# Neighbourhood attention with the scores of two heads issued together, one 512-column filler a unit, and a shorter choice chain

## The chip, the core and the metric

The kernel runs on one core of one Trainium2 chip. The metric is the device time of one execution in microseconds, from three runs of the kernel before. One more execution was recorded by the hardware profiler; the rows further down are from it. Engines are PE (TensorE), DVE (VectorE), ACT (ScalarE), POOL (GpSimd) and SP (which issues most DMAs). Each works through its own queue in order and waits on semaphores.

## The reference

The input is 2 images of 32 x 32 positions with 64 channels. Three layers follow each other:

```python
# 1: neighbourhood attention, 4 heads of 16 channels, a window of 7 x 7 keys, then an MLP
x = x + proj(softmax(q @ k_window + bias) @ v_window)
x = x + gelu(layernorm(x) @ fc1 + b1) @ fc2 + b2
# 2: global attention over 1024 tokens, 8 heads of 64
t = t + softmax(q @ k.T) @ v @ Wu + bu
# 3: 33 steps; op is the largest of the first 19 entries of token 0 of image 0
for step in range(33):
    op = argmax(h[0, 0, :19])
    h = where(attn_mask[step, op], attention(h; wq, wk, wv, wo of (step, op)), h)
    h = where(ffn_mask[step, op], relu(h @ w1 + b1) @ w2 + b2, h)
```

## The kernel before

**The neighbourhood loop.** A unit is one tile of 128 queries and one head: 2 images x 8 tiles x 4 heads = 64 units. The keys of a tile are up to 10 rows of 32 positions (320 columns; 224 for the first and last tile of an image). Each engine runs its own loop over steps i, software-pipelined by hand:

- PE, step i: `nat_score(i + 2)` (L663): wait until DVE has biased unit i (so one of the two score banks, PSUM 0 and 1, is free), one filler matmul of 256 columns (`keep_busy`, L658, L661), then two score matmuls in a 32-row group of the array (high and low part of the queries, L675). Then `nat_turn(i - 1)` (L680): wait for the exponentials, one filler, two or three 128x128 transposes of the probabilities (L688) into bank 4 for even and bank 5 for odd units. In steps 2 modulo 4 come the value sums of a tile (`nat_values`, L691, L702), in steps 0 modulo 4 the projection (`nat_project`, L707, L711), because `LAG_SUM, LAG_DRAIN, LAG_PROJ, LAG_WEIGH = 6, 7, 8, 9`.
- DVE, step i: bias and minimum of unit i in one instruction (L1520), for odd i then the copy of the transposes of unit i - 2 (L318), in steps 1 modulo 4 then the weighing of a tile's heads (L1452, L1456), and then its share of the side work.
- ACT, step i: the exponential of unit i (L1097), for even i the copy of the transposes of unit i - 2, and in steps 3 modulo 4 the copy of the value sums (L1106).

Side work stands in the same steps by a table `at_step`: on PE `x` 9, `q` 12, `k` 15, `v` 19, `wT` 24, `wk` 27, `mix` 30, `wu` 33, `y` 47, `h` 49, `H` 51, `mlp` 53 to 56, `a` 65, each drained by ACT or DVE a step or so later (10, 13, 16, 20, 25, 28, 31, 34, 48, 50, 52, 57, 66). The mean and variance of a layer norm take DVE six small instructions, one a step: steps 1 to 6, 40 to 45, and 58 to 63; POOL then raises to the power -1/2 (L1287) and DVE divides at steps 8, 46 and 64.

**The filler.** It multiplies the identity matrix, read as 16-bit numbers, by itself into a bank that is overwritten next. Its result is used by nobody.

**The global stage.** Four pairs of heads with 32 steps each (`glob_pair`); PE runs scores (L807), transposes (L820) and value sums (L834). In the first pair some work of the stage before is done beside (`rest_of_stage1`).

**The choice.** For each update of the third layer PE puts token 0 in a row of PSUM (`show_row`, L881) and `choose` (L1663) on DVE finds the operation and the next step at which a mask is set for it: twelve chained instructions, each waiting for the one before, among them two over all 33 x 19 = 627 codes (L1679, L1682), and then two that write the control words. All engines wait for these in `scan` (L370). The table of codes is made by four chained instructions (L1658 to L1661) after the last global pair, before the moments of the next layer norm. With this input there are two updates (the first an FFN alone, the second an attention and an FFN), and `choose` runs three times.

Of the kernel before, what the change touches and what calls it, by code (L numbers as in the profile page):

```python
# [67 lines left out]
NCTL = 12  # L68
# [38 lines left out]
def build(nc, a, out):  # L107
    ctx = ExitStack()
    with ctx:
# [82 lines left out]
        code = sb("code", [1, NSTEP])  # L192
        key = sb("key", [1, NSTEP])
        dead = sb("dead", [1, NSTEP])
        row = sb("row", [1, C])
# [174 lines left out]
        def scan(e, attend, feed, after):  # L370
# [13 lines left out]
            def update():  # L384
# [3 lines left out]
                slot = e.snap(nu, min_val=0, max_val=NSTEP - 1)  # L388
                if attend:
                    with e.If(flags >= 2):  # L390
                        attend(e.snap(na, min_val=0, max_val=NSTEP - 1), step, slot)
                        e.reg_add(na, na, 1)
# [63 lines left out]
        MLP_STEPS, ADD_STEP, DIVIDE_STEP, INPUT_STEP = 4, 3, 6, 7  # L456
# [78 lines left out]
        def _(pe):  # L535
# [831 lines left out]
        def _(dve):  # L1367
# [219 lines left out]
            def rest_of_stage1(i):  # L1587
# [55 lines left out]

            glob_pair(0, prev=False, beside=rest_of_stage1)
# [5 lines left out]
            cn = [0]  # L1650

            def link(ins):
                cn[0] += 1
                ins.then_inc(codes_made, 1)
                dve.wait_ge(codes_made, cn[0])
            dve.wait_ge(late_loaded, 32)
            dve.wait_ge(consts_made, 4)
            link(dve.tensor_copy(codes[:, :, :], mask8[:, 0, :, :]))  # L1658
            link(dve.tensor_copy(codew[:, :, :], mask8[:, 1, :, :]))
# [199 lines left out]
```

## Time and profile before

| | us |
|---|---|
| median of 3 runs | 726.95 |
| lowest, highest | 723.34, 731.72 |
| profiled execution | 727.6 |
| its span, first to last instruction | 725.7 |
| PE busy | 636.4 (88% of the span) |
| DVE busy | 465.6 (64%) |
| ACT busy | 386.7 (53%) |
| mean granted TensorE clock, share of 2.4 GHz | 0.939 |

Busy time counts an engine's instructions, not its waits. Matmuls are pipelined, so a PE record is longer than the time to the next record; where it matters, the distance from start to start is the one to take. A wait is put down to the instruction that came last before it ended.

### The profile page before, as it was taken

Reading aid. Unit: us, or ns where it says so; the run is one execution under the profiler, and the core shown is the slowest. Engines: PE = TensorE matmul, PEld = TensorE weight load, DVE = VectorE, ACT = ScalarE, POOL = GpSimd, SP = SyncE. Lnnn points to the kernel's source line nnn. Section 1 sums busy time; section 2 is a strip of 40 time slices with the busy share of each in tenths; the row PEclk is TensorE's granted clock in tenths of the full one; section 3 lists DMA queues with packets and bytes.
Section 4 is the critical chain, followed back from the end, with each engine's and each line's share of the span. In section 5 each row is a group of like instructions: output and inputs, shape, how many; then the busy total and the mean of one; then the engine's idle time right before and its main releaser. Section 6 shows DMA issues by size and latency. Waiting matters only on the chain.

```text
span 725.7 us, 11085 instructions
## 1 busy us (share of the span) xinstructions
PE 636.4 (88%) x3951; PEld 348.2 (48%) x3952; DVE 465.6 (64%) x799; ACT 386.7 (53%) x683; POOL 50.3 (7%) x100
## 2 busy tenths in 40 slices
PE   7999999959789999999999999999999656279961
PEld 5555655525445555555555555555555321147621
DVE  5655464553966676767677666766676454599743
ACT  3534557335666666666666666666565204355430
POOL 5021323130000000000000000000000000000000
PEclk9999999876999999999999999999999886699986
DMA  4000000000000000000000000000000000000001
GB/s 96 1 1 1 2 1 1 1 0 1 1 0 1 1 1 1 1 1 1 0 1 0 0 0 0 0 1 1 0 1 1 0 8 3 12 1 2 1 0 30
DMA packets 9509, 3.24 MB, mean 4 GB/s; under 512 B 8820, under 2 KB 9079, under 8 KB 9463
## 3 DMA queue, kind: packets, MB, share of 16 engines
q1 hardware_dynamic: 8182, 2.61, 1.6%
q8 instruction: 30, 0.49, 0.3%
q10 hardware_dynamic: 1281, 0.01, 0.1%
q14 instruction: 16, 0.13, 0.1%
HBM read 2.09 MB, written 0.52 MB: 4 GB/s over the span
## 4 chain that ended last, share of the span: by engine, by line
PE 74%; DVE 12%; issue 9%; ACT 2%; POOL 2%; DMA 1%; SPq 0%; DVEq 0%; POOLq 0%; ACTq 0%
PE PS L834 16%; PE PS L807 15%; PE PS L820 13%; PE PS L661 3%; PE PS L675 3%; PE PS L688 2%; PE PS L860 2%; PE PS L515 2%; PE PS L767 2%; PE PS L702 2%; PE PS L487 2%; PE PS L959 2%; PE PS L499 2%; DVE negm L1608 2%; PE PS L561 1%
## 5 line engine op out<-in xcount | busy, mean ns | idle before, releaser
L1608 DVE TENSOR_REDUCE negm<-PS 128x1 f32<-128x1024 f32 x128 | 156.6, 1223 | 120.2 <-PE PS L807 120.2
L1168 ACT ACTIVATE prob<-PS,negm 128x1024 f32<-128x1024 f32 x128 | 143.0, 1117 | 43.9 <-DVE negm L1608 43.9
L820 PE MATMUL PS<-ident,prob 128*128 128x128 f32 x1024 | 135.9, 274 | 10.5 <-DVE PT L1620 10.3
L820 PEld LDWEIGHTS PS<-ident,prob 128*128 128x128 f32 x1024 | 119.9, 141 | 39.0 <-DVE PT L1620 13.2
L834 PE MATMUL PS<-PT,V 128*64 128x512 f32 x512 | 134.3, 617 | 0.0
L807 PE MATMUL PS<-aS,qS 128*128 128x512 f16 x512 | 133.9, 384 | 0.0
L1180 ACT ACTIVATE PT<-PS 128x512 f32<-128x512 f32 x128 | 76.6, 598 | 106.8 <-PE PS L820 106.2
L807 PEld LDWEIGHTS PS<-aS,qS 128*128 128x128 f16 x512 | 44.7, 99 | 95.7 <-issue 52.1
L1620 DVE COPY PT<-PS 128x512 f32<-128x512 f32 x128 | 87.2, 681 | 5.2 <-PE PS L820 5.2
L1097 ACT ACTIVATE prob<-sbias,negm 128x320 f32<-128x320 f32 (+1 forms) x64 | 34.3, 537 | 38.0 <-DVE negm L1520 37.4
L1287 POOL TENSOR_TENSOR rstd<-var,minus_half 128x8 f32<-128x8 f32 x8 | 13.2, 1646 | 468.0 <-DVE var L1391 468.0
L661 PE MATMUL PS<-ident 128*128 128x256 f16 x128 | 39.3, 307 | 5.4 <-DVE negm L1520 4.1
L834 PEld LDWEIGHTS PS<-PT,V 128*64 128x64 f32 x512 | 27.3, 135 | 30.0 <-issue 29.8
L318 DVE COPY PT<-PS 128x384 f32<-128x384 f32 (+1 forms) x32 | 16.7, 523 | 33.6 <-PE PS L688 33.6
L1520 DVE CUSTOM_DVE_ANT_0 sbias<-PS,PT 128x320 f32<-128x320 f32 (+1 forms) x64 | 28.8, 459 | 7.7 <-PE PS L675 7.6
L688 PE MATMUL PS<-ident,prob 128*128 128x128 f32 x176 | 33.5, 299 | 0.0
L675 PE MATMUL PS<-k0S,q0S 32*128 32x320 f16 (+1 forms) x128 | 30.4, 322 | 0.0
L661 PEld LDWEIGHTS PS<-ident 128*128 128x128 f16 x128 | 13.1, 103 | 33.5 <-issue 16.6
L1000 ACT ACTIVATE prob<-PS,negm 128x1024 f32<-128x1024 f32 x16 | 17.8, 1115 | 20.5 <-DVE negm L1345 20.5
L1142 ACT ACTIVATE qS<-PS 128x512 f16<-128x512 f32 x36 | 21.2, 599 | 8.4 <-PE PS L767 7.9
L1168 ACT ACTIVATION_READ_ACCUMULATOR prob<-PS,negm 128x1 f32 x128 | 25.3, 198 | 0.0
L767 PE MATMUL PS<-aS,wqk 128*128 128x512 f16 x64 | 20.4, 414 | 5.0 <-DVE qS L1576 3.6
(175 smaller groups left out, 688.9 us busy)
## 6 DMA issues: line engine op xcount, KB each, us to landing
xall<-in_x_dram SPq DMA_DIRECT2D x2, 256.0 KB, 4.4
out_dram<-x SPq DMA_DIRECT2D x4, 128.0 KB, 2.1
w<-in_L_attn_Wq_dram SPq DMA_DIRECT2D x2, 128.0 KB, 2.5
w<-in_L_attn_Wk_dram SPq DMA_DIRECT2D x2, 128.0 KB, 2.6
w<-in_L_attn_Wv_dram SPq DMA_DIRECT2D x2, 128.0 KB, 2.7
fc<-in_L_conv_fc_w_dram SPq DMA_DIRECT2D x2, 64.0 KB, 2.5
wu<-in_L_attn_Wu_dram SPq DMA_DIRECT2D x2, 64.0 KB, 2.4
w1s<-in_L_ffn_ffn_w_dram SPq DMA_DIRECT2D x2, 64.0 KB, 2.1
```

The lines of the kernel that those rows point to most:

```text
L661: pe.matmul(bank[:, 0:FILL], filler[:, 0:P], filler[:, 0:FILL], start=True, stop=True)
L675: mm = pe.matmul(PS[:, u % 2, 0:rows * WW], q0S[hr, img, part, t * P:(t + 1) * P], k0S[hr, img, first * WW:(first + rows) * WW], start=(pa ...
L688: tr = pe.transpose(bank[:, n * P:(n + 1) * P], prob[:, u % 3, n * P:(n + 1) * P], ident[:, :])
L767: m = pe.matmul(bank, w.rearrange("p h a c -> p (h a c)"), aS[:, blk * BLK:(blk + 1) * BLK], start=(part == 0), stop=(part == 1))
L807: mm = pe.matmul(scores2[i % 2][:, j * BLK:(j + 1) * BLK], qS[:, part, lane, q0:q0 + P], aS[:, k0 + j * BLK:k0 + (j + 1) * BLK], start=(pa ...
L820: tr = pe.transpose(bank[:, k * P:(k + 1) * P], prob[:, u % 4, kt * P:(kt + 1) * P], ident[:, :])
L834: mm = pe.matmul(OB[cols, :], V[:, g % GP // 2 * NT + kt, cols], PT[:, g % 2, lane, kt, :], start=(kt == 0), stop=(kt == NT - 1))
L1097: act.activation(prob[:, i % 3, 0:w], sbias[:, i % 3, 0:w], ACT.Exp, bias=negm[:, i % 4:i % 4 + 1], scale=-1.0).then_inc(c0["exped"], 1)
L1168: act.activation(prob[:, i % 4, :], scores2[i % 2], ACT.Exp, bias=negm[:, i % 4:i % 4 + 1], scale=1.0, accum_out=sums[:, i // GRP, (i % GR ...
L1180: act.activation(PT[:, g % 2, lane, 0:4, qt * P:(qt + 1) * P], LO.rearrange("p (k q) -> p k q", k=4), ACT.Copy).then_inc(c1["lo_drained"], 1)
L1608: dve.tensor_reduce(negm[:, i % 4:i % 4 + 1], scores2[i % 2], AX.X, ALU.max, negate=True)\
L1620: dve.tensor_copy(PT[:, g % 2, lane, 4:8, qt * P:(qt + 1) * P], HI.rearrange("p (k q) -> p k q", k=4)).then_inc(c1["hi_drained"], 1)
```

## The change

- In the neighbourhood loop PE issues the scores of units u and u + 1 together, in steps with even i: high part of both heads, then low part of both. The heads lie in different 32-row groups and write different banks. Before them PE waits until DVE has biased both units before (`biased` >= u instead of u - 1). The filler ahead of the scores is gone.
- The filler ahead of each unit's transposes has 512 columns instead of 256.
- `choose` reads the row where it lies in PSUM, and has five chained instructions instead of twelve. It picks from a row of 19 prepared next keys (`nextkey`) instead of from all 627 codes.
- That row is made for the first choice by `key_table`, seven instructions in steps 17 to 23 of the first global pair on DVE, which also take the place of the four that made the codes after the last pair. For each later choice it is made by `keys_left`, three chained instructions on DVE (19x33 elements twice) that `scan` places at the start of every update, before its attention and FFN.

```diff
-NCTL = 12
+NCTL, NAHEAD = 5, 3
...
                 slot = e.snap(nu, min_val=0, max_val=NSTEP - 1)
+                if ahead:
+                    ahead(slot)
...
-        MLP_STEPS, ADD_STEP, DIVIDE_STEP, INPUT_STEP = 4, 3, 6, 7
+        MLP_STEPS, ADD_STEP, DIVIDE_STEP, INPUT_STEP, KEY_STEP = 4, 3, 6, 7, 17
...
-                pe.matmul(bank[:, 0:FILL], filler[:, 0:P], filler[:, 0:FILL], start=True, stop=True)
-
-            def nat_score(u):
-                T, h = u // NH0, u % NH0
+                pe.matmul(bank[:, 0:2 * FILL], filler[:, 0:P],
+                          filler.rearrange("p (o n) -> p o n", o=1).to_broadcast([P, 2, FILL]), start=True, stop=True)
+
+            def nat_scores(u):
+
+                T = u // NH0
...
                 if u >= 2:
-                    pe.wait_ge(c0["biased"], u - 1)
+                    pe.wait_ge(c0["biased"], u)
...
-                keep_busy(PS[:, u % 2, :])
-                hr = slice(32 * h, 32 * h + 32)
                 for part in range(2):
-                    mm = pe.matmul(PS[:, u % 2, 0:rows * WW], q0S[hr, img, part, t * P:(t + 1) * P],
-                                   k0S[hr, img, first * WW:(first + rows) * WW],
-                                   start=(part == 0), stop=(part == 1))
-                mm.then_inc(c0["scored"], 1)
+                    for n in range(2):
+                        hr = slice(32 * ((u + n) % NH0), 32 * ((u + n) % NH0) + 32)
+                        mm = pe.matmul(PS[:, n, 0:rows * WW], q0S[hr, img, part, t * P:(t + 1) * P],
+                                       k0S[hr, img, first * WW:(first + rows) * WW],
+                                       start=(part == 0), stop=(part == 1))
+                        if part == 1:
+                            mm.then_inc(c0["scored"], 1)
...
-            nat_score(0)
-            nat_score(1)
+            nat_scores(0)
             for i in range(UN0 + LAG_PROJ - NH0 + 1):
-                if i + 2 < UN0:
-                    nat_score(i + 2)
+                if i % 2 == 0 and i + 2 < UN0:
+                    nat_scores(i + 2)
...
+                if 0 <= i - KEY_STEP < 7:
+                    key_table(i - KEY_STEP)
...
+            def key_table(n):
...
+                if n == 0:
+                    ins = dve.tensor_copy(codes[:, :, :], mask8[:, 0, :, :])
+                elif n == 1:
+                    ins = dve.tensor_copy(codew[:, :, :], mask8[:, 1, :, :])
+                elif n == 2:
+                    ins = dve.scalar_tensor_tensor(codes[:, :, :], codes[:, :, :], 2.0, codew[:, :, :],
+                                                   ALU.mult, ALU.add)
+                elif n == 3:
+                    ins = dve.tensor_scalar(codew[:, :, :], codes[:, :, :], 0.0, float(NONE), ALU.is_equal, ALU.mult)
+                elif n == 4:
+                    ins = dve.tensor_tensor(codes[:, :, :], codes[:, :, :], steps, ALU.add)
+                elif n == 5:
+                    ins = dve.tensor_tensor(codes[:, :, :], codes[:, :, :], codew[:, :, :], ALU.max)
+                else:
+                    ins = dve.tensor_reduce(nextkey[:, :], by_op(codes), AX.X, ALU.min)
...
+            def keys_left(slot):
+
+                base = slot * (NCTL + NAHEAD) + NCTL
+                dve.tensor_scalar(dead[:, :], steps4[:, :], nextf[:, 0:1], float(NONE), ALU.is_le, ALU.mult)\
+                   .then_inc(ctl_chain, 1)
+                dve.wait_ge(ctl_chain, base + 1)
+                dve.tensor_tensor(codew[:, :, :], codes[:, :, :],
+                                  dead[:, :].rearrange("p (s o) -> p s o", o=1).to_broadcast([1, NSTEP, NOPS]),
+                                  ALU.max).then_inc(ctl_chain, 1)
+                dve.wait_ge(ctl_chain, base + 2)
+                dve.tensor_reduce(nextkey[:, :], by_op(codew), AX.X, ALU.min).then_inc(ctl_chain, 1)
+                dve.wait_ge(ctl_chain, base + NAHEAD)
...
-            link(dve.tensor_copy(codes[:, :, :], mask8[:, 0, :, :]))
-            link(dve.tensor_copy(codew[:, :, :], mask8[:, 1, :, :]))
-            link(dve.scalar_tensor_tensor(codes[:, :, :], codes[:, :, :], 2.0, codew[:, :, :], ALU.mult, ALU.add))
-            link(dve.memset(nextf[:, :], -4.0))
...
-                link(dve.tensor_copy(row[:, :], bank[0:1, 0:C]))
-                link(dve.tensor_reduce(top[:, :], row[:, 0:NOPS], AX.X, ALU.max))
+                row = bank[0:1, 0:NOPS]
+                link(dve.tensor_reduce(top[:, :], row, AX.X, ALU.max))
+
+                link(dve.scalar_tensor_tensor(cand[:, :], row, top[:, 0:1], opfrac[:, :], ALU.is_lt, ALU.add))
                 link(dve.tensor_reduce(opf[:, :], cand[:, :], AX.X, ALU.min))
-                link(dve.scalar_tensor_tensor(
-                    codew[:, :, :], opfrac[:, :].rearrange("p (o n) -> p o n", o=1).to_broadcast([1, NSTEP, NOPS]),
-                    opf[:, 0:1], codes[:, :, :], ALU.is_equal, ALU.mult))
-                link(dve.tensor_reduce(code[:, :], codew[:, :, :], AX.X, ALU.add))
...
-                link(dve.tensor_reduce(nextf[:, :], key[:, :], AX.X, ALU.min))
+                link(dve.scalar_tensor_tensor(cand[:, :], opfrac[:, :], opf[:, 0:1], nextkey[:, :],
+                                              ALU.is_equal, ALU.mult))
+                link(dve.tensor_reduce(nextf[:, :], cand[:, :], AX.X, ALU.add))
...
-            scan(dve, attend, feed, choose)
+            scan(dve, attend, feed, choose, keys_left)
```

## Rows read from the trace of the kernel before

**Rows 1.** Stretch, us: busy PE, PEld, DVE, ACT, POOL (x instructions), PEclk, DMA share, GB/s

```profile
24.00:152.00 128.00, 120.23 (x951) 67.59 (x952) 70.30 (x229) 64.08 (x136) 32.34 (x71) 0.96 0.01 1
```

**Rows 2.** Waits, 24 to 152: total us, times, longest us

```profile
DVE PT L318 <- PE PS L688: 33.6, 26, 3.1
...
PE PS L661 <- DVE negm L1520: 4.1, 9, 1.0
```

**Rows 3.** Timeline of PE, 69 to 75: start us, us, engine, line, operation

```profile
69.04 0.60 PE L711 MATMUL PS<-pw,OT 128*128 128x260 f32 x2
...
69.69 0.44 PE L675 MATMUL PS<-k0S,q0S 32*128 32x320 f16 x2
...
70.06 0.28 PE L661 MATMUL PS<-ident 128*128 128x256 f16 x1
...
70.81 0.28 PE L661 MATMUL PS<-ident 128*128 128x256 f16 x1
...
71.94 1.00 PE L702 MATMUL PS<-PT 128*32 128x128 f32 x24
...
74.49 0.28 PE L661 MATMUL PS<-ident 128*128 128x256 f16 x1
...
74.61 0.49 PE L688 MATMUL PS<-ident,prob 128*128 128x128 f32 x3
...
74.93 0.60 PE L711 MATMUL PS<-pw,OT 128*128 128x260 f32 x2
```

**Rows 4.** Timeline of DVE in the same stretch

```profile
69.25 0.56 DVE L318 COPY PT<-PS 128x384 f32<-128x384 f32 x1
...
69.72 0.17 DVE L1452 RECIPROCAL rinv<-PS 128x4 f32<-128x4 f32 x1
...
70.27 0.48 DVE L1520 CUSTOM_DVE_ANT_0 sbias<-PS,PT 128x320 f32<-128x320 f32 x1
...
70.67 0.48 DVE L1520 CUSTOM_DVE_ANT_0 sbias<-PS,PT 128x320 f32<-128x320 f32 x1
```

**Rows 5.** Timeline of PE, 33 to 43: the same score records, four units apart

```profile
33.35 0.71 PE L675 MATMUL PS<-k0S,q0S 32*128 32x320 f16 x2
...
42.62 0.71 PE L675 MATMUL PS<-k0S,q0S 32*128 32x320 f16 x2
```

**Rows 6.** A fall of the clock: timeline of PE at 135, and the stretch behind it

```profile
135.19 0.28 PE L661 MATMUL PS<-ident 128*128 128x256 f16 x1 [0.96 <-DVE negm L1520]
...
135.00:143.00 8.00, 7.81 (x51) 4.14 (x51) 3.91 (x15) 3.01 (x7) 0.30 (x1) 0.57 0.01 2
```

**Rows 7.** Timeline of PE: side matmuls on fixed rows, and on alternating halves

```profile
86.32 1.10 PE L615 MATMUL PS<-PT 64*128 64x64 f32 x8
...
90.41 0.68 PE L628 MATMUL PS<-wu,PT 64*64 64x64 f32 x16
```

**Rows 8.** Timeline of DVE: two side instructions between biases

```profile
101.82 0.69 DVE L1385 TENSOR_TENSOR xn<-xall,mean 128x512 f32<-128x512 f32 x1
...
109.31 0.95 DVE L1407 TENSOR_TENSOR xn<-xn,rstd 128x512 f32<-128x512 f32 x1 [1.37 <-POOL rstd L1287]
```

**Rows 9.** Timeline of DVE: the second choice

```profile
617.55 0.21 DVE L1673 COPY row<-PS 1x64 f32<-1x64 f32 x1 [0.63 <-PE PS L881]
...
619.34 0.80 DVE L1682 TENSOR_REDUCE code<-codew 1x33 f32<-1x627 f32 x1
...
621.63 0.14 DVE L1691 TENSOR_SCALAR control<-opf 1x1 f32 x1 [0.16 <-DVE nextf L1689]
```

**Rows 10.** Timeline, 563 to 603: the table of codes, and the first update's split

```profile
563.00 0.46 DVE L1658 CAST codes<-mask 1x627 f32<-1x627 uint8 x1
...
564.95 0.69 DVE L1381 TENSOR_REDUCE mean<-x 128x8 f32<-128x512 f32 x1
...
571.32 0.47 PE L820 MATMUL PS<-ident,prob 128*128 128x128 f32 x1 [5.93 <-DVE PT L1620]
...
602.68 0.87 DVE L1748 TENSOR_TENSOR w1S<-w1s,w1S 64x256 f16<-64x256 f32 x2 [1.94 <-ACT w1S L1227]
```

More of the change, by code:

```diff
@@ L191, in build @@
         codew = sb("codew", [1, NSTEP, NOPS])
-        code = sb("code", [1, NSTEP])
-        key = sb("key", [1, NSTEP])
         dead = sb("dead", [1, NSTEP])
-        row = sb("row", [1, C])
+        nextkey = sb("nextkey", [1, NOPS])
         top = sb("top", [1, 1])
@@ L364, in build, with scan @@
         LN2_STEP, LN3_STEP = SUM_STEP + LN + 1, at_step["mlp", 0][1] + LN + 1
-        def scan(e, attend, feed, after):
+        def scan(e, attend, feed, after, ahead=None):
             word = e.alloc_register("word")
@@ L1642, in glob_pair @@
                         beside(i)
+            by_op = lambda t: t[:, :, :].rearrange("p s n -> p n s")
+            def key_table(n):
+                if n == 0:
+                    dve.wait_ge(late_loaded, 32)
+                    dve.wait_ge(consts_made, 4)
+                else:
+                    dve.wait_ge(codes_made, n)
+                steps = steps4[:, :].rearrange("p (s o) -> p s o", o=1).to_broadcast([1, NSTEP, NOPS])
+                if n == 0:
+                    ins = dve.tensor_copy(codes[:, :, :], mask8[:, 0, :, :])
[10 more added lines that the diff above has]
+                    ins = dve.tensor_tensor(codes[:, :, :], codes[:, :, :], codew[:, :, :], ALU.max)
+                else:
+                    ins = dve.tensor_reduce(nextkey[:, :], by_op(codes), AX.X, ALU.min)
+                ins.then_inc(codes_made, 1)
+            def keys_left(slot):
[9 more added lines that the diff above has]
+                dve.wait_ge(ctl_chain, base + NAHEAD)
             glob_pair(0, prev=False, beside=rest_of_stage1)
@@ L1647, in _ @@
             glob_pair(NPAIR - 1, last=True)
[L1650 to L1657, printed above, removed]
-            link(dve.tensor_copy(codes[:, :, :], mask8[:, 0, :, :]))
-            link(dve.tensor_copy(codew[:, :, :], mask8[:, 1, :, :]))
-            link(dve.scalar_tensor_tensor(codes[:, :, :], codes[:, :, :], 2.0, codew[:, :, :], ALU.mult, ALU.add))
-            link(dve.memset(nextf[:, :], -4.0))
             def choose(now, bank=YB):
-                base = now * NCTL
+                base = now * (NCTL + NAHEAD)
                 n = [0]
@@ L1672, in choose @@
                 dve.wait_ge(row_turned, now + 1)
-                link(dve.tensor_copy(row[:, :], bank[0:1, 0:C]))
-                link(dve.tensor_reduce(top[:, :], row[:, 0:NOPS], AX.X, ALU.max))
-                link(dve.scalar_tensor_tensor(cand[:, :], row[:, 0:NOPS], top[:, 0:1], opfrac[:, :],
-                                              ALU.is_lt, ALU.add))
+                row = bank[0:1, 0:NOPS]
+                link(dve.tensor_reduce(top[:, :], row, AX.X, ALU.max))
+                link(dve.scalar_tensor_tensor(cand[:, :], row, top[:, 0:1], opfrac[:, :], ALU.is_lt, ALU.add))
                 link(dve.tensor_reduce(opf[:, :], cand[:, :], AX.X, ALU.min))
-                link(dve.scalar_tensor_tensor(
-                    codew[:, :, :], opfrac[:, :].rearrange("p (o n) -> p o n", o=1).to_broadcast([1, NSTEP, NOPS]),
-                    opf[:, 0:1], codes[:, :, :], ALU.is_equal, ALU.mult))
-                link(dve.tensor_reduce(code[:, :], codew[:, :, :], AX.X, ALU.add))
-                link(dve.tensor_scalar(dead[:, :], steps4[:, :], nextf[:, 0:1], float(NONE), ALU.is_le, ALU.mult))
-                link(dve.tensor_scalar(key[:, :], code[:, :], 0.0, float(NONE), ALU.is_equal, ALU.mult))
-                link(dve.tensor_tensor(key[:, :], key[:, :], dead[:, :], ALU.max))
-                link(dve.tensor_tensor(code[:, :], code[:, :], steps4[:, :], ALU.add))
-                link(dve.tensor_tensor(key[:, :], key[:, :], code[:, :], ALU.max))
-                link(dve.tensor_reduce(nextf[:, :], key[:, :], AX.X, ALU.min))
+                link(dve.scalar_tensor_tensor(cand[:, :], opfrac[:, :], opf[:, 0:1], nextkey[:, :],
+                                              ALU.is_equal, ALU.mult))
+                link(dve.tensor_reduce(nextf[:, :], cand[:, :], AX.X, ALU.add))
                 assert n[0] == NCTL
@@ L1709, in _ @@
                 if i == STATE_STEPS[1]:
+                    dve.wait_ge(codes_made, 7)
                     choose(0, PS[:, 2, :])
```

## The prediction

> **What bounds the kernel now.** I read the busy times by stage first. In the neighbourhood stage, 24 to 152 us, PE is busy 120.2 of 128 us and DVE 70.3 [rows 1]; the global stage is PE work too, and the change leaves its PE program alone. So the first question is whether PE waits in the neighbourhood stage, and for whom. The waits say: hardly; before its fillers it stood 4.1 us in all for the bias (DVE), while DVE stood 33.6 us in 26 waits for the transposes before its copies [rows 2]. PE is the bound there, with DVE close behind.
>
> The timeline of PE and of DVE over four units (one key tile: one projection, one value sum) shows how close [rows 3, 4]. From projection to projection 5.89 us pass. A filler with its transposes holds PE 0.44 (74.49 to 74.93); a score pair takes 0.37 until the next filler starts (69.69 to 70.06). On DVE, copy to next instruction is 0.47, the two head-weighing instructions take 0.55, and two biases follow each other at 0.40 and last 0.48.
>
> **The neighbourhood loop, part by part.** Before, a unit's PE work is filler, scores, filler, transposes. Now steps with i even issue the scores of two heads at once, and only turns carry a filler, twice as long. The number of filler columns stays. What changes is the wait: the pair may start only when DVE has biased both units before it, so the two banks are never one ahead of the other. I follow one block of four units (i = 0 to 3 modulo 4, from the moment the bias of unit i+1 is done); DVE's copy of an odd unit stands before the next bias in its queue, and the transposes it needs now stand behind the new scores in PE's.
>
> First leg, i = 0: release 0.06 (the first bias ends at 70.75, the filler that waits for it starts at 70.81), scores 0.42, transposes done after a longer filler 0.12 + 0.11 + 0.49 = 0.72, DVE copy 0.47 starting at 1.24. The projection starts on PE at 1.04 and is ready at 1.64, DVE weighs from 1.71 to 2.26, two biases (0.40 + 0.48 + a short read-out, 0.91) end at 3.17. Second leg, i = 2: 0.06 + 0.42 + 0.72 + 0.04 + copy 0.47 + biases 0.91 = 2.62; PE meanwhile does scores 0.48, turn 0.66, values about 0.95, turn 0.56 = 2.65. Together 5.8, against 5.9 before [rows 3, 4]. At the high clock I count the block of bare units as 0: PE's saving turns into a PE gap of about 1.0 us in the first leg, and DVE with its hand-over becomes the bound.
>
> At the low clock the same legs give 4.4 + 3.9 = 8.3 us (streaming counted twice: scores 0.64, turn 1.05, projection 0.86, values 1.0) where the block takes 9.27 (33.35 to 42.62; the score record is 0.71 there and 0.44 later [rows 3, 5]). Three such blocks: -3.0.
>
> Side work on PE that stands in steps 0 or 1 modulo 4 now falls into the 1.0 us gap: folded values (0.68), weight turning, one hidden block, two quarters of the MLP, each between that and the 1.10 of the mixing or longer [rows 7]; five at 0.85, as the gap allows: -4.2. The query projections are there too, but DVE waits for them at once: 0.
>
> Side work on DVE is the counterpart. Before, an instruction of moments, drains or divides between two biases hid under PE if it stood in step 2, 3 or 0; now each such instruction delays a pair. The moments are busy 0.69 each, of which the next instruction overlaps a little, the drains 0.8; I take 0.65 as the mean. I count sixteen large ones by the step tables (moments 3, 4, 42, 43, 44, 58, 60, 62; divides 8, 46; drains 10, 16 twice, 20 twice, 48): 16 x 0.65 = 10.4. The wait of 1.37 for POOL at step 46 now stands in the path too: 11.8 [rows 8]. Less 1.8 that PE already stood for them (4.1 of rows 2, less about 0.28 in eight blocks): +10.0.
>
> Loop: -3.0 - 4.2 + 10.0 = +2.8. Bounds: DVE's part fully hidden -7; fully added with no gain from gaps +12.
>
> Do the two heads really overlap? The trace has no two score records in different row groups. Nearest: the sixteen 64x64 matmuls that alternate between both halves of rows and columns take 0.68 in all, 0.04 each, where eight on fixed rows take 1.10, 0.14 each [rows 7]. So disjoint parts overlap; I take full overlap (0.42), and no overlap (0.42 + 0.27) as the other end, 0.27 = 2 x 320 columns at 2.4 GHz. The Trainium skill (TensorEngine Tiling (Array Packing), Key Properties) says that tiles in different rows can load weights and multiply in parallel and that changing the tiling mode drains the engine; with it the scores would be the 0.42 taken. The same page (PSUM Bottleneck) warns that tiling speeds up TensorE but not the PSUM evacuation, which may become the bound; that speaks against the change, and the legs above are how I read it here.
>
> **The choice chain.** Before, row copy to control word is 617.55 to 621.63 less 0.16, about 3.95 us. After: reduce 0.24 from PSUM, compare 0.27, reduce 0.19, a 19-wide select 0.26, reduce 0.19 = 1.15 [rows 9]. It runs three times; the first lies beside PE's last global value sums (0), the other two are alone on the path: 2 x 2.8 = -5.6. Reading the row in PSUM twice instead of once may cost 0.1 each; bound -5.0.
>
> What was left out of the chain comes back as three instructions at the start of each update, ahead of all DVE work: 0.27 + 0.83 + 0.83, plus waits and register work, 2.1 (the 627-element reduce is 0.80 [rows 9]; its new order of reading is unmeasured, between 0.80 and 1.6). In the first update DVE goes from its register work straight to the split of the FFN weights at 602.68, which PE waits for [rows 10]: +2.1. In the second update DVE stands for the loaded attention weights anyway: 0, at worst +2.1.
>
> The four instructions that made the code table stood at 563.00, before the moments at 564.95, and PE's next transposes at 571.32 waited 5.93 us for DVE behind them [rows 10]: -1.9. They move as seven instructions, about 4.7 us, to steps 17 to 23 of the first global pair, one a step of some 3 us in which PE is bound and DVE about two thirds busy: 0, at worst +1.5. Tail: -5.6 + 2.1 - 1.9 = -5.4.
>
> **Sum.** The profiled execution took 727.6 us (span 725.7), the median is 726.95, so the two can be read as one. 727.6 + 2.8 - 5.4 = 725.0.
>
> **Rivals.**
> - A, the clock falls in the gaps. PE now stands about 1.0 us in each block, more where DVE has side work in steps 1 and 2 (1.4 more at 57/58 and 61/62). Before, the granted clock fell to the 1.2 GHz level right after a stand of 0.96 us at 135.19, and averaged 0.57 over the next 8 us [rows 6]. A block costs 8.3 at the low level and 5.9 at the high: 2.4 more. If some 45 us are low, 45 / 8.3 x 2.4 = +13: 738. It decides (slower by 1%) from about 32 us of low clock. Against: fillers per turn are denser than before, and 47 to 135 us stayed high in spite of nine stands.
> - B, the row groups do not overlap: 32 pairs x 0.27 = +8.6: 733.6, slower but just within 1%.
> - C, the high clock comes early. Before, PE ran some 22 us at the low level though it never stood [rows 5]. The new PE stream is denser between its gaps. Three blocks at 5.9 rather than 8.3: -7, 718.
> - D, the side work on DVE hides after all (drains of other steps absorb it): 725 - 8 = 717.
> - E, the shortened choice isn't shorter on the path: the three returned instructions cost in both updates, with a slow reduce: +3: 728.
>
> **Chances.** Forecast with E 0.42 (720 to 732); A 0.20; B 0.13; C 0.15; D 0.10. The range leaves out the far ends of A and of C with D together: 714 to 742; the likeliest case by itself 720 to 732. A measurement of this kernel tells about 1% from no change, 719.7 to 734.2: faster 0.26 (C, D, a sliver), slower 0.27 (A, part of B), same 0.47.
>
> **What would show it.** In the neighbourhood stage: PE waits before the scores for the bias, about once a block, some 1 us and in all 15 to 30 us instead of 4.1; four score records followed by a filler within 0.45 (0.7 means B); DVE's waits for the transposes stay near 1 us. Score and filler records at the low level past 47 us mean A, at the high level before 40 mean C. The choice should take 1.2 us of DVE from first to last reduce; PE's stand at 571 should shrink to 4.0, the first FFN matmul should come 2.1 later against the state's turn. I am wrong above all if side work on DVE doesn't add, or if the clock goes another way.

## The result: 1.1% slower

| | before | after |
|---|---|---|
| median of 20 runs each, same chip, us | 723.51 | 732.33 |
| lowest, highest | 721.18, 731.75 | 727.91, 741.05 |
| ratio after / before | | 1.0111, 95% [1.0083, 1.0140] |
| profiled execution (its span) | 727.6 (725.7) | 730.34 (728.4) |
| PE busy | 636.4 | 619.6 |

Ratios here and below leave out the executions that lie over 1.5 per cent above the fastest of their kernel, the medians hold all, and so a ratio and the quotient of two medians differ by up to half a per cent.

I had forecast a gain of 2 us, to 725.0; measured is a loss of 8.8 between the medians. The time itself lies within 714 to 742, but the direction and the size do not match, and the loss is just beyond the 1% that I had called no change.

How the two profiled executions run apart, by the same places of the program (start, us; "behind" is after less before):

| place | before | after | behind |
|---|---|---|---|
| first matmul of the loop (a filler before, scores after) | 24.25 | 24.33 | +0.1 |
| first global projection piece (end of the neighbourhood stage) | 152.64 | 160.70 | +8.1 |
| moments after the global stage | 564.95 | 570.91 | +6.0 |
| first FFN matmul | 604.30 | 613.40 | +9.1 |
| second choice: first reduction | 617.79 | 626.26 | +8.5 |
| its control word | 621.63 | 627.50 | +5.9 |
| end of the span | 725.7 | 728.4 | +2.7 |

All that is lost is lost in the neighbourhood stage. Behind it the steps of the short choice come out as they were summed (below), but for 0.7 us between the moments and the first FFN matmul, where eight transposes took 1.81 us (581.92) for 1.10 before (575.98). One caution on this pair: the profiled execution of before is one of its longer ones, 4 us above its median, and that of after is 2 us below its own. So the stage's +8.1 understates the loss.

The neighbourhood stage of after, the view of [rows 1], with the stage's whole length (24 to 160.7) as a second row:

```profile
24.00:152.00 128.00, 100.76 (x827) 61.04 (x827) 63.39 (x213) 60.05 (x128) 26.92 (x62) 0.92 0.00 1
24.00:160.70 136.70, 106.19 (x889) 64.33 (x889) 69.50 (x229) 63.12 (x136) 31.79 (x71) 0.93 0.01 1
```

PE was busy 120.23 of 128 us; now it is 100.76, and over the whole, longer stage 106.19. It has some 14 us less to do and needs 8 us more for it. The clock is 0.92 where it was 0.96. The waits of the stage (24 to 162 us), the view of [rows 2], say where the time stands:

```profile
DVE PT L316 <- PE PS L691: 52.3, 30, 6.5
...
PE PS L677 <- DVE negm L1522: 25.3, 20, 3.5
```

PE's wait for the bias went from 4.1 us to 25.3, and DVE's wait for the transposes from 33.6 to 52.3. Each engine waits more for the other: neither is the bound, the hand-over between them is.

The score pair, in the timeline of PE (answering [rows 3]):

```profile
73.77 0.49 PE L691 MATMUL PS<-ident,prob 128*128 128x128 f32 x3
74.19 0.44 PE L677 MATMUL PS<-k0S,q0S 32*128 32x320 f16 x4
74.56 0.39 PE L661 MATMUL PS<-ident 128*128 128x512 f16 x1
74.79 0.49 PE L691 MATMUL PS<-ident,prob 128*128 128x128 f32 x3
75.12 0.60 PE L714 MATMUL PS<-pw,OT 128*128 128x260 f32 x2
```

Four score matmuls, then the filler 0.37 later (74.19 to 74.56), the distance that two took before (69.69 to 70.06, [rows 3]). The two row groups overlap fully. Rival B is out by this row.

### The profile page after: what moved, and what is told of

Same layout as the page of the kernel before. It is cut to its first block, busy times and chain, and to the rows that moved or that the text cites. A ratio compares the mean times of both kernels' runs of the same rounds, so it can differ in the third digit from the quotient of the medians.

```text
span 728.4 us, 10937 instructions
## 1 busy us (share of the span) xinstructions
PE 619.6 (85%) x3887; PEld 344.9 (47%) x3888; DVE 464.2 (64%) x787; ACT 385.0 (53%) x683; POOL 49.7 (7%) x100
## 4 chain that ended last, share of the span: by engine, by line
PE 70%; DVE 14%; issue 9%; ACT 3%; POOL 2%; DMA 1%; DVEq 0%; SPq 0%; POOLq 0%; ACTq 0%
PE PS L836 15%; PE PS L809 15%; PE PS L822 13%; PE PS L691 2%; PE PS L661 2%; PE PS L862 2%; PE PS L515 2%; PE PS L769 2%; DVE sbias L1522 2%; DVE negm L1612 2%; PE PS L677 2%; PE PS L487 2%; PE PS L499 2%; PE PS L705 2%; PE PS L561 1%
## 5 line engine op out<-in xcount | busy, mean ns | idle before, releaser
L822 PEld LDWEIGHTS PS<-ident,prob 128*128 128x128 f32 x1024 | 120.5, 142 | 37.4 <-DVE PT L1624 11.6
L316 DVE COPY PT<-PS 128x384 f32<-128x384 f32 (+1 forms) x32 | 16.8, 524 | 52.3 <-PE PS L691 52.3
L677 PE MATMUL PS<-k0S,q0S 32*128 32x320 f16 (+1 forms) x128 | 15.4, 322 | 25.8 <-DVE negm L1522 25.3
L691 PEld LDWEIGHTS PS<-ident,prob 128*128 128x128 f32 x176 | 26.7, 159 | 8.7 <-issue 3.7
L661 PE MATMUL PS<-ident 128*128 128x512 f16 x64 | 28.3, 443 | 1.2 <-ACT PT L316 0.8
L1170 ACT ACTIVATION_READ_ACCUMULATOR prob<-PS,negm 128x1 f32 x128 | 25.3, 197 | 0.0
L1578 DVE SCALAR_TENSOR_TENSOR qS<-PS,qS 128x512 f16<-128x512 f32 x36 | 24.3, 682 | 0.4 <-ACT qS L1144 0.3
```

Of the source, the lines that this page charges most:

```text
L661: pe.matmul(bank[:, 0:2 * FILL], filler[:, 0:P], filler.rearrange("p (o n) -> p o n", o=1).to_broadcast([P, 2, FILL]), start=True, stop=True)
L677: mm = pe.matmul(PS[:, n, 0:rows * WW], q0S[hr, img, part, t * P:(t + 1) * P], k0S[hr, img, first * WW:(first + rows) * WW], start=(part = ...
L691: tr = pe.transpose(bank[:, n * P:(n + 1) * P], prob[:, u % 3, n * P:(n + 1) * P], ident[:, :])
L822: tr = pe.transpose(bank[:, k * P:(k + 1) * P], prob[:, u % 4, kt * P:(kt + 1) * P], ident[:, :])
L1170: act.activation(prob[:, i % 4, :], scores2[i % 2], ACT.Exp, bias=negm[:, i % 4:i % 4 + 1], scale=1.0, accum_out=sums[:, i // GRP, (i % GR ...
```

## Experiments

The kernels of one group ran on one chip together with before; each ratio is to the runs of before beside it.

### Which part loses: one part alone

`e1` is before with the new attention order and filler, and the old choice. `e2` is before with the new choice alone. `e4` is before with only the filler's part:

```diff
 def nat_score(u):
     ...
-    keep_busy(PS[:, u % 2, :])
     ...
 def keep_busy(bank):
-    pe.matmul(bank[:, 0:FILL], filler[:, 0:P], filler[:, 0:FILL], start=True, stop=True)
+    pe.matmul(bank[:, 0:2 * FILL], filler[:, 0:P], filler.rearrange("p (o n) -> p o n", o=1).to_broadcast([P, 2, FILL]), start=True, stop=True)
```

`e3` is the changed kernel with one swap, so that the older unit's turn doesn't queue behind the pair's wait:

```diff
-    if i % 2 == 0 and i + 2 < UN0:
-        nat_scores(i + 2)
     if 1 <= i <= UN0:
         nat_turn(i - 1)
+    if i % 2 == 0 and i + 2 < UN0:
+        nat_scores(i + 2)
```

> The kernel before with the new score and filler part only, the choice as before. If the loss is all in the neighbourhood loop, this is slower than the full change: the loop's +8.0 us of the profiled executions and nothing given back, ratio to before 1.011 to 1.018. If the parts only cost together (rival: the clock falls because both move work), it is near 1.00 to 1.005.

> The kernel before with the choice part only. From the profile after: -2.8 for each of two choices, -1.9 for the code table, +2.4 for the three instructions ahead of the first update: -5.1 us, ratio 0.993. If the seven instructions in the first global pair or the three in the second update cost something, it is 0.996 to 1.00.

> The kernel after, with PE issuing in each even step the transposes of unit i - 1 before the two score pairs instead of behind them; nothing else is moved. Hand-over theory (DVE's copy of the odd unit waits for transposes that stand behind scores that wait for DVE's bias): both legs lose about 1.2 us of waiting, PE's waits before the scores fall from 25 us to under 8, DVE's before its copies from 52 to under 15, and the loop gets 12 to 20 us shorter: ratio to before 0.975 to 0.99. Clock theory (the loss is only the stretches at the low clock): the order of the issues matters little, ratio 1.00 to 1.015.

> The kernel before with the filler part only: 512 columns ahead of each unit's transposes, none ahead of the scores; scores one head at a time as before. Filler theory (the fillers' new place costs the clock): low-clock stretches appear between 47 and 135 us and the time grows, ratio above 1.005. Hand-over theory: the filler's place is no cause; PE saves the switch of the array ahead of each score pair, about 0.1 us a unit in a loop that PE bounds, 0 to -7 us, ratio 0.99 to 1.00.

| kernel | median | ratio to before | 95% |
|---|---|---|---|
| e1, new attention alone | 738.49 | 1.0179 | 1.0125 to 1.0233 |
| e2, new choice alone | 718.69 | 0.9923 | 0.9888 to 0.9959 |
| e4, filler alone | 718.90 | 0.9927 | 0.9901 to 0.9952 |
| e3, changed kernel, turn first | 715.15 | 0.9860 | 0.9813 to 0.9908 |

The parts add up: 1.0179 x 0.9923 = 1.0101, against 1.0111 for both. The choice gives 5.6 us, as summed. The attention costs 12.9 us where I had +2.8. Inside it the filler gives 5.3, so pairing the scores with its wait costs 1.0179 / 0.9927 = 1.025, about 18 us. And it is the order of turn and wait that costs: with the turn ahead of the wait, e3 comes to 0.986, which is within its interval what filler and choice give by themselves (0.9927 x 0.9923 = 0.985).

The waits fell less than I had expected. PE's wait for the bias came down from 25.3 to 13.3 us (expected under 8), DVE's for the transposes from 52.3 to 24.5 (under 15):

```profile
DVE PT L316 <- PE PS L691: 24.5, 14, 6.3
...
PE PS L677 <- DVE negm L1522: 13.3, 17, 2.9
```

The clock isn't what helped e3: over its loop (24 to 147.45) the mean is 0.90, below the 0.93 of the changed kernel.

### Does DVE's side work stand in line now, and did it not before?

`e5` and `e6` add the same work to before and to after, in steps 2 modulo 4:

```diff
+    if i < UN0 and i % 4 == 2:
+        dve.memset(scratch[:, :], 0.0)
```

> The kernel before, with one more instruction of DVE in every fourth step of the attention loop: a memset of 128x512 into a tile that nobody reads, 16 in all, ahead of the step's side work. Its length is taken as about 0.6 us, so some 9 us of added DVE work. Theory 'hand-over' (DVE's side work costs time only where TensorE has nothing but DVE's next result to go on with): before, every unit's scores have their own step of lead, TensorE waited for the bias 9 times for 4.1 us, so most of the 9 us disappear: 0 to +3 us (ratio 1.000 to 1.004). Rival 'DVE in line everywhere': +9 us (1.012), here as in the changed kernel. Rival 'DVE's side work never adds': 0 in both.

> The changed kernel with the same 16 memsets. Hand-over: the pair's scores wait for DVE, with the older unit's turn queued behind them, so the 9 us stand in line: +6 to +9 us over the changed kernel, 1.019 to 1.023 of the kernel before if the changed one stands at 1.011. Rival 'DVE's side work never adds': 1.011, and the loss of the change is then of the clock or of the order alone.

Groups of instructions by line on DVE in e6, with busy us and mean ns: the added work.

```profile
L1528 DVE MEMSET scratch<- 128x512 f32 x16 | 7.8, 485 | 0.9
```

Before with it: 722.75, ratio 1.0004 [0.9975, 1.0032]. After with it: 737.87, ratio 1.0203 [1.0160, 1.0246]. So 7.8 us of DVE work at this place are free in before, to within 2 us, and in after they cost 0.9 per cent, 6.7 us, known to about 4. The waits of PE for the bias show the same, first e5, then e6:

```profile
PE PS L662 <- DVE negm L1521: 4.0, 9, 1.0
```

```profile
PE PS L678 <- DVE negm L1523: 28.9, 20, 3.5
```

Before's row hasn't moved with 7.8 us more to do (4.1 in [rows 2]); after's rose from 25.3 to 28.9. A part of the 6.7 may be the clock, since the profiled loop of e6 has 0.88 for 0.93. One stretch of the loop is free of that: from tile 7's projection to tile 10's, with three of the memsets in it, first e5, then e6:

```profile
93.14:112.32 19.18, 17.83 (x164) 9.99 (x163) 14.79 (x46) 9.89 (x22) 6.10 (x13) 1.00 0.00 1
```

```profile
104.88:131.68 26.80, 16.28 (x152) 9.68 (x151) 15.34 (x47) 10.52 (x22) 6.09 (x13) 0.94 0.00 1
```

The same stretch takes 19.18 without the memsets in before's order and 25.80 at 0.93 in after (both rows stand below). So the old order hides all three, and of the 1.31 us that DVE does more in the new one 1.00 shows.

`e10` and `e11` go the other way: in both kernels the two reductions and the square of each set of moments in the loop are cut to 64 of 512 columns.

```diff
+    m = 1 if k in (2, 3, 4) else NT
-    ins = dve.tensor_tensor(xsq[:, :, :], buf, buf, ALU.mult)
+    ins = dve.tensor_tensor(xsq[:, 0:m, :], buf[:, 0:m, :], buf[:, 0:m, :], ALU.mult)
```

> The kernel before, where nine of DVE's side instructions in the attention loop (the two reductions and the square of the three sets of moments) do only the first 64 of their 512 columns, 0.68 us each before, about 0.15 then: some 4.8 us of DVE work left out, and the output is not the reference's. Hand-over theory: 0 to -2 us (0.997 to 1.000), as this work lies beside TensorE's. Rival (DVE is in line before too): -4.8 us, 0.993.

> The changed kernel with the same nine instructions cut to 64 columns (the output is not the reference's). Hand-over theory: the pair's wait passes DVE's side work on, so -3.5 to -5 us against the changed kernel, 1.004 to 1.006 of the kernel before if the changed one stands at 1.011. If the work hides, 1.011. If its absence also keeps the clock up, more than -5 us, below 1.004.

As whole times these two can't be compared: the wrong means reach the choice, and other updates are done, so that they take 657.67 and 660.10 us. What can be read is a stretch of the loop. In the same stretch, tile 7's projection to tile 10's (steps 36 to 48), lie three of the shortened instructions. It took, in e2 (before's order) and in e10:

```profile
95.11:114.29 19.18, 17.83 (x164) 9.99 (x163) 13.54 (x43) 9.83 (x22) 6.10 (x13) 1.00 0.00 1
```

```profile
90.28:109.47 19.19, 17.84 (x165) 10.01 (x164) 12.34 (x43) 9.74 (x22) 6.11 (x13) 1.00 0.00 1
```

and in after and e11:

```profile
93.65:119.45 25.80, 16.23 (x152) 9.48 (x151) 14.03 (x44) 10.48 (x23) 6.09 (x13) 0.93 0.01 1
```

```profile
96.21:120.65 24.44, 16.28 (x153) 9.68 (x151) 12.61 (x44) 10.21 (x23) 6.10 (x13) 0.93 0.01 1
```

DVE's busy time falls by 1.20 in the old order and the stretch stays at 19.2; in the new one it falls by 1.42 and the stretch by 1.36. At equal clocks in each couple that is the same answer as e5 and e6: side work is hidden in the old order and stands in line, nearly whole, in the new one. Not everywhere, though: e10's first projection came at 39.81 instead of 41.41, so the early moments had cost before something too.

### How much of it is the clock?

After's stretch from tile 11's projection to tile 13's, and the same work in e11 and e2:

```profile
127.89:151.13 23.24, 19.18 (x135) 13.64 (x133) 9.14 (x29) 10.01 (x19) 2.82 (x8) 0.71 0.00 1
```

```profile
129.08:146.05 16.97, 12.98 (x135) 9.23 (x133) 8.57 (x29) 9.99 (x19) 3.16 (x8) 1.00 0.00 1
```

```profile
123.91:139.69 15.78, 14.60 (x142) 9.80 (x141) 9.12 (x29) 8.93 (x18) 3.16 (x8) 1.00 0.01 2
```

At a granted clock of 0.71 it took 23.24 us, at 1.00 in the same order 16.97, of which one shortened instruction (0.6) explains little. So the low clock cost some 5.5 us in this one stretch, and the order itself 1.2 to 1.8 (16.97, and the 0.6 with it, against 15.78). Two experiments put more filler work on PE. `e7` issues two fillers a turn in place of one, ahead of the wait for the exponentials. `e12` leaves the turn as it is and fills the stands before the pairs:

```diff
 def nat_scores(u):
+    if u >= 4:
+        pe.wait_ge(c0["hi_drained"], (u - 3) // 2)
+        for _ in range(10 if u == 48 else 2):
+            keep_busy(HI)
     if u >= 2:
         pe.wait_ge(c0["biased"], u)
```

> The changed kernel, with the filler of a turn issued ahead of its wait for the exponentials (only the bank's drain is waited for), and two of them in place of one: TensorE works about 0.2 us more a unit, 13 us in all, in time in which it stood, and the order of all other work stays. Theory 'clock' (the loss of the change is that TensorE stands 25 us and loses its high clock at 68, 112 and 133 us): the low stretches of about 30 us between 68 and 150 us go, and with them 4 to 8 us: ratio to the kernel before 1.000 to 1.005. Theory 'hand-over' (the loss is time in which TensorE waits for DVE): the waits stay at 20 to 25 us, ratio 1.008 to 1.014; if TensorE turns out to be in line, the added 13 us bring it above 1.014.

> The changed kernel, with two further 512-column fillers (0.43 us at the high level) issued ahead of each pair's wait for DVE, and ten at step 46, where TensorE stood 3.48 us: they go into the bank whose drain the turn behind the pair waits for anyway, so what the pair and the turn wait for is as before, and TensorE works in 25 us of stands that it had. Clock theory (low-level stretches behind the stands, 127.89 to 151.13 us at 0.71 above all, cost about half of the loss): the mean clock of the loop rises from 0.93 to 0.97 or more and 4 to 6 us come back: 1.003 to 1.006 against the kernel before. Hand-over alone: the clock may rise, but the time stays at 1.009 to 1.013. If DVE's bias comes earlier than the fillers end in many blocks, they stand in line themselves: up to 32 x 0.4 us, and the ratio is above 1.015.

| kernel | median | ratio | 95% | loop's mean clock, profiled |
|---|---|---|---|---|
| after | 732.33 | 1.0111 | 1.0083 to 1.0140 | 0.93 |
| e7, two fillers a turn | 732.90 | 1.0130 | 1.0092 to 1.0167 | 0.92 |
| e12, fillers in the stands | 725.15 | 1.0019 | 0.9993 to 1.0046 | 0.98 |

e12 gives 0.9 per cent back, 6.6 us, known to about 3, and its twelve runs lie within 724.46 and 728.26, where after's twenty spread from 727.91 to 741.05. This is net of what the added fillers cost where PE didn't stand: from tile 10's projection to tile 11's, at 1.00 in both, e12 takes 9.51 and after 8.44. The same stretches in e12 (tile 7 to 10, 11 to 13, and the loop):

```profile
93.47:117.80 24.33, 19.07 (x172) 10.70 (x171) 14.02 (x44) 10.36 (x23) 6.08 (x13) 1.00 0.00 1
...
127.31:145.60 18.29, 16.11 (x142) 10.36 (x141) 9.04 (x29) 9.06 (x18) 3.15 (x8) 0.91 0.01 1
24.00:155.46 131.46, 111.17 (x957) 63.40 (x958) 69.22 (x229) 63.06 (x136) 32.21 (x71) 0.98 0.01 1
```

The second stretch is 4.95 us shorter than in after, at 0.91 for 0.71. The first is only 1.47 shorter although its clock is full: 24.33 against 19.18 of before's order, and those 5.15 us are the hand-over. e7 had 12.4 us more busy PE time in its loop and no better time. Its profiled execution, the longest of its six, shows no better clock in the loop; over whole executions its clock was higher, 0.936 to 0.945 in the six against 0.916 to 0.939 in after's twenty. So the fillers in the turns did raise the clock, and what that gave went into their own time: from tile 10's projection to tile 11's, at 1.00 in both, e7 takes 9.30 for 8.44, and its stands before the pairs were still 21.2 us, where e12's were 16.6. Where the filler stands counts, not only how much of it there is.

### Is there a version that beats both?

`e8` takes the filler and the choice, keeps the old order of scores, and makes the keys behind the choice rather than at the head of an update. `e9` is e3 with that move of the keys. `e13`, `e14` and `e15` add fillers before the pairs to e9: two each, one each (both ten at step 46), or ten at step 46 alone, in bank LO behind ScalarE's drain of it.

```diff
     dve...control words...then_inc(control_ready, 1)
+    keys_left(now)
 ...
-scan(dve, attend, feed, choose, keys_left)
+scan(dve, attend, feed, choose)
```

> The kernel before with its attention order, one 512-column filler in each turn and none ahead of the scores, the short choice, and the three operations that make the next keys put behind the choice instead of at the head of an update. Expected from the two parts alone (0.9927 and 0.9923): 0.985; the moved keys take up to 2.4 us from the head of the first update, if DVE is free behind the choice until the update's first data come: 0.982. If the two parts share their gain (both move the same later wait) it is 0.990; if the keys only move from one place in line to another, 0.985.

> The changed kernel with two moves: the older unit's turn is issued ahead of a pair's scores and their wait (as in e3_turn_first, 0.9860), and the keys are made behind the choice. If pairing in row groups is worth something once its wait holds nothing up, this beats the filler alone with the same choice (0.9851): below 0.980. If pairing is only neutral: 0.984 to 0.988. In e8 the moved keys gave nothing beyond the sum of the two parts, so 0 is expected of them here.

> e9_turn_first_keys_behind (0.9826, mean clock of the loop 0.90) with two fillers ahead of each pair's wait, ten at step 46, in the bank that the next turn uses, behind that bank's drain. Clock theory: half of e12's gain or more, as this order stands 13 us and not 25 in its waits: 0.974 to 0.979. If the drain (ScalarE's copy) comes later than DVE's bias, the pairs wait for it and the ratio is above 0.985. What tells the theories apart: e12 gave 0.9 per cent from clock alone; if the clock was the rest of e9's cost over a high-level loop as well, the loop's clock rises to 0.96 or more here and the time falls with it; if it was particular to the changed order, nothing comes.

> The same with one filler ahead of each pair's wait (ten at step 46). If two are more than the stands hold (14 stands were seen for 31 pairs), this is faster than e13 at the same clock, by up to 31 x 0.21 = 6.5 us; if one is too little for the clock, slower: 0.980.

> e9_turn_first_keys_behind with fillers at one place only: ten of 512 columns ahead of the pair's wait at step 46, where the same order (e3_turn_first) stood 2.92 us and ran at the low level behind it. If that stand costs the clock that e9 lacks (0.90 in its loop), the loop's clock rises to 0.95 or more, and the time falls to 0.972 to 0.979; if other stands do it as well, it stays at 0.981 to 0.985.

| kernel | median | ratio | 95% |
|---|---|---|---|
| e8, old order, filler, choice, keys behind | 712.33 | 0.9851 | 0.9814 to 0.9888 |
| e9, turn first, keys behind | 710.41 | 0.9826 | 0.9778 to 0.9873 |
| e13, two fillers before each pair | 724.42 | 1.0013 | 0.9978 to 1.0048 |
| e14, one filler before each pair | 722.81 | 0.9944 | 0.9899 to 0.9989 |
| e15, ten at step 46 only | 710.31 | 0.9831 | 0.9803 to 0.9859 |

e13 and e14 lost in the way that the expectation of e13 names. The clock was high, 0.99 over 24 to 150 us in both, but PE now waited for ScalarE ahead of the fillers (12.5 us in e14). Waits of e13, 24 to 156 us:

```profile
PE PS L661 <- ACT PT L316: 12.7, 14, 1.8
```

The drain of LO comes later than the bias that the fillers were to wait for. With one filler for two e14 is 0.7 per cent faster than e13, 5 us, so they also cost by themselves. e15 raised the loop's clock from 0.90 to 0.93, less than the 0.95 I had expected, and the time stayed within both intervals. So e8, e9 and e15 can't be told apart; all three are some 1.5 to 1.7 per cent below before and 2.6 to 2.8 below the changed kernel. The old order with the long filler (e8) gets there without pairs, and its six runs lie closest together (710.56 to 713.25). The moved keys gave nothing that shows: e8 is at 0.9851, and the product of filler and choice is 0.985.

That e3 equals the filler and the choice alone is a sum of a gain and a loss, not two nothings. The projection of tile 7 starts at 82.75 in e3 and at 88.58 in e4, and at 83.91 in e9 for 88.61 in e8. Of these 5.8 and 4.7 us, 1.9 come between tile 0's projection and tile 7's, with the score records at the high level in all four, and the rest earlier, where the pairs reach that level sooner (score records at 0.44 us from 30.96 and 36.41, against 38.61). Then the pairs lose it all, and more in these executions. The stretches from tile 7 to 10 and from tile 11 to 13, first in e3, then in e4:

```profile
82.75:105.61 22.86, 17.57 (x152) 10.70 (x150) 14.24 (x45) 10.75 (x24) 6.11 (x13) 0.85 0.01 1
114.24:136.11 21.87, 19.20 (x135) 13.66 (x133) 9.17 (x30) 9.87 (x19) 2.83 (x8) 0.69 0.00 1
```

```profile
88.58:107.22 18.64, 17.17 (x153) 9.28 (x152) 13.55 (x43) 9.85 (x22) 6.10 (x13) 1.00 0.01 2
116.50:132.50 16.00, 14.62 (x134) 9.64 (x133) 9.13 (x29) 9.25 (x19) 3.15 (x8) 1.00 0.01 2
```

The profiled executions of e3 and e9 are their longest. The shortest of e9, 706.21 and 707.62 at a mean clock of 0.950 and 0.951, lie 3 to 4 us below the shortest of e8, 710.56 at 0.949. That points to a gain of a few us from pairing where the clock stays high and no ready turn is queued behind its wait; two runs don't show it, and no kernel here held that clock in every run.

## Why the prediction was wrong

**The choice part was right, step by step.** From first reduction to control word the second choice took 3.84 before (617.79 to 621.63) and takes 1.24:

```profile
626.26 0.17 DVE L1705 TENSOR_REDUCE top<-PS 1x1 f32<-1x19 f32 x1 [0.66 <-PE PS L883]
...
627.17 0.16 DVE L1711 TENSOR_REDUCE nextf<-cand 1x1 f32<-1x19 f32 x1
627.50 0.14 DVE L1713 TENSOR_SCALAR control<-opf 1x1 f32 x1 [0.16 <-DVE nextf L1711]
```

With the row copy (0.24) left out as well, that is 2.8 saved, the term as forecast. PE's stand behind the code table shrank from 5.93 [rows 10] to 3.97, the 4.0 that I had named:

```profile
577.27 1.11 PE L822 MATMUL PS<-ident,prob 128*128 128x128 f32 x4 [3.97 <-DVE PT L1624]
```

and from the end of the neighbourhood stage to 564.95 / 570.91 the lag falls by 2.1, so the moved table is hidden in the global stage (1.9 forecast). The keys at the head of the first update cost about 2.4 for 2.1, since the reduction in its new order of reading took 1.30 and not 0.80:

```profile
608.67 0.80 DVE L1681 TENSOR_TENSOR codew<-codes,dead 1x627 f32<-1x627 f32 x1
609.50 1.30 DVE L1685 TENSOR_REDUCE nextkey<-codew 1x19 f32<-1x627 f32 x1
```

In the second update they lie in the time for which DVE would stand anyway: from control word to the end 103.9 us passed before (621.75 to 725.7, second word), and 100.8 after (627.61 to 728.4), which is the third choice's saving and no loss. Sum forecast -5.4; e2 measured -5.6 (-3.0 to -8.1).

**The neighbourhood loop failed**, +2.8 forecast and +12.9 measured (e1, 9.0 to 16.8). Its terms:

- *Clock, -3.0 (three early blocks at the low level).* This is the term with the wrong sign, and the largest miss. The early blocks gained half a microsecond and lost it again: the first three projections came at 40.95, 47.81 and 59.56; in e2, with before's order, at 41.41, 48.36 and 58.34. The legs at the low level had promised more: from the scores of unit 4 to those of unit 8 the new order took 7.91 (27.49 to 35.40) and before's 6.75 (28.42 to 35.17), from unit 8 to 12, with side work in both, 8.87 (35.40 to 44.27), and e2 9.28 (35.18 to 44.46). The profiled before had the second at 50.42, since it stayed at the low level longer than its sisters: my three slow blocks were a trait of that one execution. What I gave to rival A, a clock that falls in the new stands, happened: low-level stretches about 68 to 71, 112 to 116 (right behind the longest stand), 133 to 143 and 146 to 150 us. Not every fall needs such a stand: e2, in the old order, shows a clock of 0.52 over 66 to 73 us, where PE hadn't stood since 60.79, and there for 0.23 us. The longest new stand, and the DVE work that caused it:

```profile
112.21 0.51 PE L677 MATMUL PS<-k0S,q0S 32*128 32x320 f16 x4 [3.48 <-DVE negm L1522]
```

```profile
108.94 0.48 DVE L1522 CUSTOM_DVE_ANT_0 sbias<-PS,PT 128x320 f32<-128x320 f32 x1
...
110.80 0.94 DVE L1409 TENSOR_TENSOR xn<-xn,rstd 128x512 f32<-128x512 f32 x1 [1.37 <-POOL rstd L1289]
111.67 0.48 DVE L1522 CUSTOM_DVE_ANT_0 sbias<-PS,PT 128x320 f32<-128x320 f32 x1
```

  e12 prices the clock at 6.6 us, with a loop at 0.98; before's own loop had 0.96 and e2's 0.97, so a part of the 6.6 may be low clock that the old order has as well. So the term was up to about +6.6 where I had -3.0. The evidence I used against A, nine stands before 135 us that left the clock high, is miscounted: the ninth of [rows 2] and the longest, 0.96, is the one at 135.19 behind which the clock fell, and the eight before it are 0.8 us and less. The new ones are 20, up to 3.5 us. I had the stands in my own sum (1.0 us a block and more) and let the old ones speak for them.
- *PE side work in the gap, -4.2.* Right in kind, too large. From tile 10's projection to tile 11's the stretch took 8.44 for e2's 9.62, from tile 4's to tile 5's 7.09 for 7.78; with the blocks between I find 2 us in all, and e4 had 9.28 and 7.56 there, so a part of it is the filler's. PE work is hidden only as long as the pair is what PE waits for.
- *DVE side work, +10.0.* Right in kind: e6 shows 6.7 of 7.8 us in line by the whole times and 1.00 of 1.31 in the stretch at like clocks, and e5 shows that the same work was free before. The two together gave +5.8 at the high clock, and e12, which is the new order with the clock kept up, is 1.0019 / 0.9923 = 1.0097 over e2, +6.9, known to about 3. The wait for POOL at step 46 is in line as summed: the stand that it caused was 3.48.
- *Bare block 0.* About right: from tile 6's projection to tile 7's it took 5.31 for e2's 5.42; the block that the legs were worked out on (69.04 to 74.93 before, 5.89) took 6.15 in e12 at the full clock.

So the step that failed is the clock term: -3.0 forecast, up to +6.6 measured, nearly the whole distance between +2.8 and +12.9. At the high clock my legs came within about 1 us of the measured loop, closer than its interval of 3 us can show, and partly by luck: I passed over the filler's part with "the number of filler columns stays". e4 shows that one long filler in place of two short ones, and none ahead of the scores, is worth 5.3 us by itself. My legs held that gain without naming it, and so hid what pairing costs: 18 us against the same kernel without it.

**The rivals.** A was the nearest by mechanism, priced at 738 and right in the place (the stands) but at about half its size. B and D fell (row 74.19 to 74.56; e6). C didn't come in the changed kernel: the high level was reached at about 41 us, and e2, in the old order, had it at 42.6. E happened only in its slow reduction, 0.5 us. Of the signs I had named, PE's wait before the scores came (25.3 us, 15 to 30 forecast), and DVE's waits for the transposes did not stay near 1 us (30 of 1.7 on the mean, the longest 6.5).

**PSUM.** The warning that tiling can move the bound to the evacuation of PSUM (TensorEngine Tiling (Array Packing), PSUM Bottleneck, in the Trainium skill) fits the waits here in part: PE had 14 us less to do and its wait for DVE, which reads the scores out of PSUM, grew by 21. But DVE was busy 69.5 of 136.7 us, and one swap of the order took 12 us of that wait away (13.3 in e3): the read-out didn't become the bound, the order of the hand-over did. I read it into the legs at the high clock and not into what the stands do to the clock.

## What to carry to other kernels

Where an engine in a hand-ordered loop waits for the slower partner, look at what is queued behind the wait: here one swap, the ready turn ahead of the scores that must wait, was worth 2.5 per cent, and the overlap of row groups nothing on average, since its early gain went into a clock that fell later. When a change frees TensorE in a stage, price the clock with the new stands in it and not by the old ones, and if the stands stay, fill them at the place where it stands, behind a drain that is certainly over. Test the parts of a bundle alone: the long filler and the short choice were each worth 0.7 to 0.8 per cent, and were hidden by the part that lost.

## What the runs showed of the chip that I had not expected

- Four 32-row matmuls of 320 columns in two row groups go through in the time of two in one group: 0.37 us from the first record to the next instruction (74.19 to 74.56 after, 69.69 to 70.06 before).
- The same stretch of work in the same order took 16.97 us at a granted clock of 1.00 and 23.24 at 0.71 (0.6 of it another instruction). How much of an execution is at the low level differs from one to the next: ten of after's twenty lie within 727.91 and 731.12 at a mean clock of 0.925 to 0.939, and three from 737.63 to 738.51 at 0.917 to 0.922, where e12, with the stands filled, spans 3.8 us in twelve at 0.942 to 0.947.
- In before until 46.15 us and in after until 39.41 the score records last 0.71 us each, and 0.44 later, while the granted clock reads 1.00 over 24 to 41 us in both; the view by windows doesn't show a start like this one, the records do.
- A reduction of 627 elements on one partition took 1.30 us when the inner index runs over the 33 steps with a stride of 19, and 0.80 when it runs over 19 neighbours [rows 9].
